# Fused state-space layer and ternary-weight FFN on 8 cores: the mixing of the next token quarter moved into the normalisation loop, and one multiply of the second quantiser moved from VectorE to GpSimd

## The reference

```python
# x: 8 x 2048 x 2048
Bu = x @ gB.T                      # real and imaginary part, 256 states
h[t] = A * h[t-1] + Bu[t]          # complex recurrence over the tokens
y = Re(C h) + D * x
x = layernorm(x + y)
h = rmsnorm(x) * norm_w
gv = act_quant(h) @ ternary(w_gv).T        # 2048 -> 2 * 8192
h = value * silu(gate)
h = act_quant(h) @ ternary(w_out).T        # 8192 -> 2048
x = layernorm(x + (x + h))
```

## Time and profile before

| | |
|---|---|
| median of 2 runs | 6203.79 us (6185.49 to 6222.1) |
| the profiled execution | 6211.08 us |
| its span, slowest core (core 5) | 6209.5 us |
| spans of the 8 cores | 6104.5 to 6209.5 us |
| busy: PE, PEld | 3524.5 us (57%), 1343.6 us (22%) |
| busy: DVE, ACT, POOL | 2416.8 us (39%), 1403.6 us (23%), 1018.0 us (16%) |
| mean granted TensorE clock, slowest core | 0.795 |

### The profile page before, as it was taken

One profiled execution on the slowest core, in us unless ns is written; L12 is line 12 of the kernel. 1 busy time (PEld: TensorE's weight loads), 2 busy tenths in 40 slices (PEclk: granted clock), 3 DMA queues, 4 the chain that ended last, 5 costly groups with the idle time before them and its releaser, 6 DMA issues.

```text
span 6209.5 us, 44092 instructions; the slowest of 8 cores (6104.5 to 6209.5 us)
## 1 busy us (share of the span) xinstructions
PE 3524.5 (57%) x13489; PEld 1343.6 (22%) x13489; DVE 2416.8 (39%) x3369; ACT 1403.6 (23%) x1134; POOL 1018.0 (16%) x933
## 2 busy tenths in 40 slices
PE   1223313302767766777777799737773674476274
PEld 0100000000323222333333334313221221122121
DVE  1333543736222222332222333387573466157100
ACT  2221112032344433444444433100000000000000
POOL 0110000000111111111111122101112211321324
PEclk9756756655888888898888899859886787788686
DMA  8232333256555535554555543124442443344233
GB/s 230 88 108 81 105 142 142 92 185 178 161 159 156 164 104 121 145 149 146 148 149 146 144 116 85 39 63 131 119 131 81 116 124 96 109 127 114 92 106 103
DMA packets 457458, 774.82 MB, mean 125 GB/s; under 512 B 24412, under 2 KB 323583, under 8 KB 423943
## 3 DMA queue, kind: packets, MB, share of 16 engines
q1 hardware_dynamic: 333096, 276.98, 16.8%
q0 software_dynamic: 68832, 243.32, 13.2%
q10 hardware_dynamic: 55296, 251.68, 12.0%
HBM read 662.83 MB, written 117.44 MB: 126 GB/s over the span
## 4 chain that ended last, share of the span: by engine, by line
DMA 33%; PE 22%; DVE 18%; issue 11%; ACT 9%; POOL 7%; DVEq 1%; ACTq 0%; SPq 0%; POOLq 0%
DMA P<-wgvT 7%; PE psA L982 7%; DMA WR<-wq2sp 5%; DMA WOF<-wgvT 5%; DMA WR<-wgvT 5%; PE psA L781 5%; PE psB L781 4%; DMA WOF<-woutT 3%; ACT HBF L733 3%; DMA WR<-woutT 3%; POOL CBF L801 2%; DMA CBF<-x1sp 2%; DVE HBF L793 2%; PE psB L982 2%; DMA CBF<-h2sp 2%
## 5 line engine op out<-in xcount | busy, mean ns | idle before, releaser
L982 PE MATMUL psA<-P,WR 128*128 128x512 bf16 x3072 | 775.8, 414 | 508.6 <-DMA WR<-wq2sp 405.7
L781 PE MATMUL psA<-P,CBF 128*128 128x512 bf16 x2048 | 509.8, 409 | 272.9 <-DVE CBF L806 257.2
L781 PE MATMUL psA<-P,MNA 128*128 128x512 bf16 x2048 | 509.4, 409 | 234.1 <-DVE CBF L806 224.6
L982 PEld LDWEIGHTS psA<-P,WR 128*128 128x128 bf16 x3072 | 312.8, 104 | 1001.6 <-issue 719.9
L801 POOL TENSOR_TENSOR CBF<-HBF,P 128x1024 f32<-128x1024 f32 x128 | 299.3, 2339 | 1334.4 <-ACT HBF L798 1221.9
L781 PE MATMUL psB<-P,MNA 128*128 128x512 bf16 x2048 | 457.4, 379 | 9.6
L781 PE MATMUL psB<-P,CBF 128*128 128x512 bf16 x2048 | 457.4, 379 | 9.6
L971 POOL DMA_DIRECT2D WR<-wq2sp x256 | 228.9, 895 | 1011.5 <-PE psA L982 759.7
L781 PEld LDWEIGHTS psA<-P,CBF 128*128 128x128 bf16 x2048 | 208.4, 104 | 573.1 <-issue 379.7
L781 PEld LDWEIGHTS psA<-P,MNA 128*128 128x128 bf16 x2048 | 208.3, 104 | 533.8 <-issue 339.9
L798 ACT ACTIVATE HBF<-HBF 128x1024 f32<-128x1024 f32 x128 | 135.3, 1057 | 769.1 <-DVE HBF L793 769.1
(11 more groups left out here) (213 smaller groups left out, 4204.6 us busy)
## 6 DMA issues: line engine op xcount, KB each, us to landing
P<-wgvT SPq DMA_DIRECT2D x128, 1024.0 KB
WR<-wq2sp POOLq DMA_DIRECT2D x256, 512.0 KB, 5.3
WOF<-wgvT ACTq DMA_DIRECT2D x64, 1024.0 KB, 4.6
WR<-wgvT ACTq DMA_DIRECT2D x64, 1024.0 KB, 4.6
WOF<-woutT SPq DMA_DIRECT2D x64, 1024.0 KB
h2sp<-CBF POOLq DMA_DIRECT2D x128, 256.0 KB, 5.3
WOF<-woutT ACTq DMA_DIRECT2D x32, 1024.0 KB, 5.2
WR<-woutT ACTq DMA_DIRECT2D x32, 1024.0 KB, 5.0
```

The costliest lines, as they stand in the source:

```text
L781: sv=sv, last=last: t.matmul(PS[:, (vg * 2 + tq) * 512:(vg * 2 + tq + 1) * 512], WQap(sv + vg)[:, a * 128:(a + 1) * 128], P1[:, a * T + th ...
L982: seg=seg, PSm=PSm: t.matmul(PSm(ds), WR[:, sl * 2048 + jj * 256 + ds * 128: sl * 2048 + jj * 256 + (ds + 1) * 128], P1[:, seg * 16384 + j ...
```

## The change

The change has three parts.

1. In stage B, `emit_xload` is called for a quarter of P2 at a time, within the normalisation loop, and `emit_mix_a(q + 1, a - 4)` stands in that loop for a = 4 to 15. The quantisation loop keeps the mixing steps 12 to 15, behind its first four tiles. SP's list is the same as before: four loads of x, then the loads of the quantisation.
2. Four row broadcasts of stage B use psA banks 2 and 3, since psB banks 2 and 3 now collect the sums of the next quarter at that time.
3. In stage D, the first multiply of `d_chain` is an instruction of POOL.

```diff
@@ -517,14 +517,14 @@
     MX1, MN1 = MXA[:, 0:512], MXA[:, 512:1024]
     RMX1, RMN1 = [("MXA", 0)], [("MXA", 1)]
 
-    def emit_xload(q):
-        for part in range(4):
-            lo = part * 4
-            b.dma("sync", lambda s, q=q, lo=lo: s.dma_start(
-                out=P2.ap().rearrange("p (a t) -> p a t", a=DT)[:, lo:lo + 4, :],
-                in_=xT_h.rearrange("(a p) t -> p a t", p=128)[:, lo:lo + 4,
+    def emit_xload(q, lo=0, n=16):
+        for part in range(lo // 4, (lo + n) // 4):
+            pl = part * 4
+            b.dma("sync", lambda s, q=q, pl=pl: s.dma_start(
+                out=P2.ap().rearrange("p (a t) -> p a t", a=DT)[:, pl:pl + 4, :],
+                in_=xT_h.rearrange("(a p) t -> p a t", p=128)[:, pl:pl + 4,
                                                               q * 512:(q + 1) * 512]),
-                writes=R("P2", lo * 512, (lo + 4) * 512))
+                writes=R("P2", pl * 512, (pl + 4) * 512))
 
     def emit_mix_a(q, a):
         bank = a % 2
@@ -592,8 +592,8 @@
              reads=R("rows", 1024, 1536) + [("srow", 0)], writes=R("rows", 1024, 1536))
         b.op("vector", lambda v: v.reciprocal(rs(2), rs(2)),
              reads=R("rows", 1024, 1536), writes=R("rows", 1024, 1536))
-        bcast_row(repr_(0), [("REP", 0)], PSB(2), RB(2), REP[:, 0:512], [("REP", 0)])
-        bcast_row(repr_(1), [("REP", 1)], PSB(3), RB(3), REP[:, 512:1024],
+        bcast_row(repr_(0), [("REP", 0)], PSA(2), RA(2), REP[:, 0:512], [("REP", 0)])
+        bcast_row(repr_(1), [("REP", 1)], PSA(3), RA(3), REP[:, 512:1024],
                   [("REP", 1)])
         for a in range(DT):
             k = a % 2
@@ -628,8 +628,11 @@
                     MN1, OTS[:, k * 512:(k + 1) * 512], colNW[:, a:a + 1], MN1,
                     OP.mult, OP.min),
                     reads=[("OTS", k), ("colNW", 0)] + RMN1, writes=RMN1)
-        if q + 1 < NQ:
-            emit_xload(q + 1)
+            if q + 1 < NQ:
+                if a % 4 == 3:
+                    emit_xload(q + 1, a - 3, 4)
+                if a >= 4:
+                    emit_mix_a(q + 1, a - 4)
         b.op("vector", lambda v: v.tensor_scalar(MN1, MN1, -1.0, None, OP.mult),
              reads=RMN1, writes=RMN1)
         b.op("vector", lambda v: v.tensor_tensor(MX1, MX1, MN1, OP.max),
@@ -660,12 +663,12 @@
              reads=R("rows", 0, 512), writes=R("rows", 512, 1024))
         b.op("vector", lambda v: v.tensor_scalar(rs(1), rs(1), QB, None, OP.mult),
              reads=R("rows", 512, 1024), writes=R("rows", 512, 1024))
-        bcast_row(rs(0), R("rows", 0, 512), PSB(3), RB(3),
+        bcast_row(rs(0), R("rows", 0, 512), PSA(3), RA(3),
                   dqa1rep[:, q * 512:(q + 1) * 512],
                   R("P3", q * 512, (q + 1) * 512), scale=1.0 / QB)
         b.op("vector", lambda v: v.tensor_tensor(rs(2), rs(2), rs(1), OP.mult),
              reads=R("rows", 512, 1536), writes=R("rows", 1024, 1536))
-        bcast_row(rs(2), R("rows", 1024, 1536), PSB(2), RB(2),
+        bcast_row(rs(2), R("rows", 1024, 1536), PSA(2), RA(2),
                   SREP, [("MXA", 3)])
         for a in range(DT):
             k = a % 2
@@ -680,8 +683,8 @@
                 reads=[("OTS", k), ("colNW", 0), ("MXA", 3)], writes=src_regs)
             round_neg(k, P1[:, a * T + q * 512:a * T + (q + 1) * 512],
                       R("P1", a * T + q * 512, a * T + (q + 1) * 512, es=2))
-            if q + 1 < NQ:
-                emit_mix_a(q + 1, a)
+            if q + 1 < NQ and a < 4:
+                emit_mix_a(q + 1, 12 + a)
         for ci in range(50 + q * 20, min(NGV, 70 + q * 20)):
             emit_abs_chunk(wgv_chunk(ci), ci)
 
@@ -941,7 +944,7 @@
             reads=[("h2sp", jo, q // 2)],
             writes=R("CBF", hq * 512, (hq + 1) * 512, es=2))
         src_ap, src_regs = RN[hsl][0], RN[hsl][1]
-        b.op("vector", lambda v, hq=hq, src_ap=src_ap, par=par: v.tensor_tensor(
+        b.op("gpsimd", lambda g, hq=hq, src_ap=src_ap, par=par: g.tensor_tensor(
             src_ap, CBF[:, hq * 512:(hq + 1) * 512], S2B[par],
             OP.mult),
             reads=R("CBF", hq * 512, (hq + 1) * 512, es=2) +
```

## The result

| | before | after |
|---|---|---|
| median | 6188.13 us of 10 runs (6165.2 to 6268.02) | 6581.19 us of 11 runs (6564.32 to 6733.83) |
| ratio after / before, 95% interval | | 1.062 [1.0582, 1.0657] |
| busy DVE, POOL (slowest core) | 2416.8, 1018.0 us | 2383.8, 1320.9 us |
| square root to square root in stage B, core 5 | 264.0, 262.0, 262.3 us | 223.5, 219.7, 219.3 us |

The change costs 393 us. In some executions the cores of one die run some per cent longer at a lower granted clock, whatever the kernel; readings here are of executions and cores without that, and in the profiled execution of after (spans 6537.8 to 6736.1 us) that is core 5. Core 5 is also the core whose rows stand ahead of the prediction.

What follows compares the result with a forecast made beforehand. No single engine was taken to bound the kernel: transfers hold a third, PE 22%, DVE 18%. 283 + 93 + 149 + 34 - 130 = +429 on the profiled 6211.08 gave 6640, so a median of 6633 us, range 6440 to 6770.

Steps and rivals of the forecast that it cites:

- Stage B, -130: Stage B: with mixing moved, chunks start earlier beside other work; cycle 262.0 to 218.7 us, three times, -130 us.
- Half 1, 24 groups, +283: Stage D, half 1, quarters 0 to 2: weights issued behind four multiplies, PE starts at 24.1 not 12.3 us; +283.
- the way from issue to start: Stage D, half 1: time from POOL's issue of the weights to PE's start, taken as 6.26 us.
- the two buffers: Stage D chains: POOL's third multiply must wait, since it writes the buffer that chain 1 still reads.
- Half 0 of quarter 0, +93: Stage D: 32 multiplies stand ahead of the first weights, then groups take 27.35 us; half 1 starts later, +93 us.
- Later halves 0, +149: Stage D, half 0 of quarters 1 to 3: groups of 40.6 or 36.2 us; +49.8 us each, +149 in all.
- the chain beside a multiply: Stage D: DVE's chain with POOL's multiply behind its first cast takes 4.42 us, against 4.05 before.
- PE's pace, +34: Stage D, half 1: after gaps grown to 24 us PE's matmuls run slower, 1.4 us x 24 = +34 us.
- No exclusion: Rival, chance 0.20: POOL and DVE do not lock each other out, a chain is 3.26 us; +253, 6457 us.
- Free multiplies: Rival, chance 0.08: POOL's multiplies fit in PE's wait for the output step in stage D; 5998 or 6074 us.
- The 20 us for descriptors: Stage D: DVE's casts in two-port mode keep POOL from writing transfer descriptors; an estimated 20 us more, outside the sum.

Runs made afterwards that it cites:

- experiments without chunks: Kernel before, and the same with parts 1 and 2 alone, both without stage B's 78 chunk sums: 5970.51 and 6004.86 us.
- four-buffer run: Changed kernel with the product of POOL's multiply in four buffers in turn, not two: 6545.9 us, recorded ratio 1.0575; the one comparable run 1.038.
- memset run: Changed kernel with POOL's multiply replaced by a write of ones into the same buffer, same waits: 6612.05 us in one run.
- run with paired loads: Changed kernel with four product buffers and both loads of neighbouring tiles emitted ahead of the first one's multiply: 6414.0 us; the one comparable run 1.016.

## Why the prediction was right

Predicted 6633, measured 6581; slower by 6.2% where 0.90 stood on slower. Point by point:

- **Stage B, -130.** Measured -125.8. The cycle of 218.7 came as 219.3 to 223.5. Two errors cancelled: the chunks take 109.5 us and not 102.5, for which I hold the loads and stores of the other tiles beside them; the way to them, square root to last Square, takes 110.2 and not 116.2. The experiments without chunks show the mechanism itself.
- **Half 1, 24 groups, +283.** Measured +263 in the gaps. PE's end to POOL's issue was 17.9 us in the group shown, 17.8 predicted, and PE's start 23.7 against 24.1. Over the 24 gaps the mean went from 11.9 to 22.8 us. The mis-sized term is the way from issue to start, taken at 6.26 from the earlier trace rows: it was 5.1 to 5.8 us after. The 6.26 was not the transfer's time, because PE was still at its matmuls of ones (the row at 4360.19). So "POOL's place in its own list decides when PE goes on" was a misreading of the kernel before, where the weights had about 1.7 us to spare (11.9 - 4.9 - 5.3, an estimate from these rows); the change made it true. Also, the single waits were not all those of the working: before the second multiply POOL waited 2.59 us for the load, which I had at nothing. The group came out right, by luck, because that product was ready at 4300.87, and was not needed before chain 1 had ended at about 4303, so DVE's work set the time either way.
- **Why POOL waits.** The prediction named the two buffers. The four-buffer run shows that this is half of the cause: behind it stood the load, through dependences in 2 KB pieces. The prediction had these loads at nothing, though the trace of before showed DVE's multiply waiting for them 59 times, 63.8 us in all.
- **Half 0 of quarter 0, +93.** Measured +90.3 with the first group of half 1. Two errors cancelled here: PE's first weight matmul came 129.9 us after the first multiply (3861.1 to 3991.0) and not 141.5, and from there to the start of half 1 it took 235.1 us and not 228.0. **Later halves 0, +149:** measured +132.2. The mis-sized term in both is the chain beside a multiply, taken at 4.42 us. It is 4.02 (3875.06 to 3879.08 in the rows below), since the multiply starts while the first cast still runs. Ahead of PE's first matmul that is 29 x 0.4 = 11.6 us. In a later half 0 the working has 16 such steps ahead of the tail (4 in the first group, 3 in each of the next four), 6.4 us too many, and 5.7 show in each.
- **PE's pace, +34.** This step failed: about 10 us came. I took one pair of rows (9.72 us after 21 us of idling) as the rule for gaps of 24. In half 1 the growth was 273.1 / 24 = 11.4 us a group, of which 11.0 are the gap. From first to last matmul, 18 of 21 groups took 17.9 to 18.8 us, as before (17.3 to 18.9); three, the one shown above among them, took 20.7 to 21.1. A later group of the same half:

```profile
4481.18 8.52 PE L985 MATMUL psA<-P,WR 128*128 128x512 bf16 x32 [11.20 <-DMA WR<-wq2sp]
4492.08 7.07 PE L985 MATMUL psA<-P,WR 128*128 128x512 bf16 x32 [2.38 <-DMA WR<-wq2sp]
```

That group takes 15.6 us of matmuls behind a gap of 22.9 us. Whether 32 matmuls took 7.1, 8.5 or 9.8 us was not set by the length of the gap ahead alone: the granted clock in the rows of 9.84, 8.52 and 7.07 us was 0.71, 0.83 and 1.00.
- **The sum.** Stage D was overestimated by 63 us (559 against 495.7): 24 for PE's pace, 20 in the gaps of half 1, 17 in the later halves 0 and 3 in quarter 0. With stage B that makes +370 on core 5, where +429 was predicted; the medians differ by 393, and that they come closer is not to the prediction's credit.
- **No exclusion,** the rival of 6457 us. Its premise fell: the engines do lock each other out (next section). Its 247 + 34 + 68 + 34 = 383 us for stage D, with a chain of 3.26, stand beside 387 in the memset run, with a chain of 3.46, but that agreement is partly luck: half 1 has 266 there, half 0 of quarter 0 with the first group 53, the later halves 0 the predicted 68, and the 34 for PE's pace filled the rest. By the memset run the lock-out and the longer operation were worth 109 us, and the larger part of the loss would have come without them.
- **Free multiplies,** the faster rival. It needed buffers that were free when POOL came. In the run with paired loads they are, and the halves 1 are still 43 to 50 us longer than before: PE's wait for the output step does not hide POOL's four multiplies, since they stand behind that step and ahead of the weights. So it would not have come true with free buffers either: that kernel is at 1.016 of the kernel before, with the gain of stage B in it.
- **The 20 us for descriptors,** the estimate after the Trainium skill (SBUF — State Buffer, SBUF: two separate sides), left out of the sum: POOL's issue of a weight transfer has a median of 0.88 us before and after. No run here shows such a cost.

## What to carry to other kernels

An engine that issues the critical engine's transfers delays them by everything that stands ahead of them in its list, and a wait there counts in full: 303 us more of busy time on POOL cost 8.4%, and the same work behind two transfers instead of ahead of them about half of that. Before moving work to an "idle" engine, list what is queued behind each moved instruction and who needs it. When a wait is taken away, look for the second one behind it, and check in what pieces the dependences are counted. And before a wait is called the bound, look at the row just ahead of the engine's restart: here it was another one that ended last, until the change.

## What the runs showed of the hardware

A multiply on POOL and DVE's chain do hold each other up, but less than an instruction's length is lost. The timelines of DVE and POOL of the kernel after in half 0 of quarter 0:

```profile
3875.06 0.42 DVE L247 CAST MNA<-MNA 128x512 int32<-128x512 f32 x1
3875.58 1.20 DVE L249 CAST MNA<-MNA 128x512 f32<-128x512 int32 x1
3876.88 0.69 DVE L251 TENSOR_TENSOR MNA<-MNA 128x512 f32<-128x512 f32 x1
...
3879.08 0.42 DVE L247 CAST CH_I<-CH_HS 128x512 int32<-128x512 f32 x1
```

```profile
3875.29 1.21 POOL L947 TENSOR_TENSOR CH_HS<-CBF,REP 128x512 f32<-128x512 bf16 x1 [3.17 <-DVE P L257]
```

The second cast, 0.43 us when POOL is idle, waits for the multiply and is booked at 1.20: 0.77 us a chain, for 1.21 us of POOL's work. L251, with its two inputs in this memory, is stretched in the same way where a multiply has already begun, from 0.69 to 1.46 (the row at 4299.95 above). Who starts second waits: a cast begun at 4507.47, 0.07 us ahead of a multiply, took its usual 0.42, and the multiply took 1.36. The memset, which only writes, stretched the cast to 0.64 and left L251 at its 0.69, in all 15 that began beside a running memset (the pair at 4043.70 above), and was itself 0.68 long beside DVE against 0.52 alone. The Trainium skill (SBUF — State Buffer, Who interferes with whom) states that a VectorE instruction with two inputs in this memory contends with a GpSimd instruction that reads it, and not with one that only writes it. By that rule, the traces agree.

This is also why DVE's busy time fell by only 33 us, though 256 multiplies of 0.69 us (176 us) left it: the stretched casts took most of it back.

POOL's multiply takes 1.15 to 1.18 us with a bf16 input while DVE idles, up to 1.58 beside DVE, and 1.26 with two inputs of f32 in the rows above. The last surprise was PE: over the 246 us of half 1 of quarter 1 before, its granted clock was 0.83, and over the 328 us of the same half after, 0.74, though from first to last matmul its groups took 18.3 us in both. The lower level (0.50) fell on the matmuls of ones, 1.86 us for two at 4294.13 above, against 1.02 in other such gaps, and on parts of the gaps.
